# Products of the unit matrix on TensorE between the routing and the first expert

## The reference

```python
h = _layernorm(x) * (1 + ca) + sa
x = x + ga * attention(h)                       # 8 heads, softmax over 1024 positions
h = _layernorm(x) * (1 + cb) + sb
logits = h_flat @ router_w.T                    # 4096 tokens, 8 experts
chosen_e = argmax(softmax(logits)); chosen_p = max(softmax(logits))
pos = cumsum(onehot)[chosen_e] - 1              # place of the token in its expert's rows
kept = pos < 768
buf[chosen_e, pos] = h_flat * kept
hh = gelu(buf @ w1[e] + b1[e])                  # 768x256 by 256x1024
eo = hh @ w2[e] + b2[e]                         # 768x1024 by 1024x256
x = x + gb * eo[chosen_e, pos] * chosen_p * kept
```

## Time and profile before

| | |
|---|---|
| time, median of 3 runs | 975.81 us (975.32 to 976.56) |
| the profiled execution's own time | 975.42 us |
| its span, first to last instruction | 973.7 us |
| PE busy | 865.9 us, 89% of the span |
| DVE, ACT, POOL busy | 670.3, 563.6, 607.0 us |
| mean granted clock of TensorE | 0.943 |
| TensorE idle in one piece at the border of blocks three and four | 25.9 us, to 685.34 us |

### The profile page before, as it was taken

One profiled execution on the slowest core, in us unless ns is written; L12 is line 12 of the kernel. 1 busy time (PEld: TensorE's weight loads), 2 busy tenths in 40 slices (PEclk: granted clock), 3 DMA queues, 4 the chain that ended last, 5 costly groups with the idle time before them and its releaser, 6 DMA issues. The chain is left out here.

```text
span 973.7 us, 20139 instructions
## 1 busy us (share of the span) xinstructions
PE 865.9 (89%) x7974; PEld 605.8 (62%) x7974; DVE 670.3 (69%) x1266; ACT 563.6 (58%) x968; POOL 607.0 (62%) x438
## 2 busy tenths in 40 slices
PE   4895899999999999999999979860799999999995
PEld 1351366666666666666666758760476777677764
DVE  4767887878887878887888609843276567565743
ACT  3641476767676767676767745653447545644650
POOL 5200388888888888888888974786324533452342
PEclk9995699999999999999999989965799999999998
DMA  9911000000000000000000014378434534353110
GB/s 276 335 68 33 1 1 2 3 2 2 2 1 2 2 2 3 2 2 2 2 2 3 2 51 162 120 260 277 145 107 135 183 101 162 129 172 103 43 52 20
DMA packets 52368, 72.32 MB, mean 74 GB/s; under 512 B 11618, under 2 KB 44583, under 8 KB 52048
## 3 DMA queue, kind: packets, MB, share of 16 engines
q1 hardware_dynamic: 42322, 53.93, 16.8%
q0 software_dynamic: 7680, 16.87, 5.3%
q10 hardware_dynamic: 2272, 0.24, 0.2%
HBM read 46.76 MB, written 29.67 MB: 78 GB/s over the span
## 5 line engine op out<-in xcount | busy, mean ns | idle before, releaser
L809 POOL TENSOR_TENSOR prob_lo<-prob 128x1024 f16<-128x1024 f32 x208 | 390.4, 1896 | 120.4 <-ACT prob L781 119.9
L833 DVE TENSOR_REDUCE part_max<-x_ps 128x1 f32<-128x512 f32 x512 | 325.2, 681 | 79.0 <-PE x_ps L730 75.7
L781 ACT ACTIVATE prob<-st_ps 128x512 f32<-128x512 f32 x512 | 281.6, 595 | 114.4 <-PE st_ps L718 108.6
L730 PE MATMUL x_ps<-KX,CQ 98*128 98x512 f16 x512 | 205.0, 405 | 4.0 <-DVE KX L845 1.4
L718 PE MATMUL st_ps<-CQ,KX 99*128 99x512 f16 x512 | 197.2, 386 | 2.8 <-ACT prob L781 1.5
L1304 POOL DMA_INDIRECT out<-yo,xb x48 | 47.7, 994 | 153.4 <-DVE yo L1411 148.5
L756 PE MATMUL acc_ps<-VV,prob 128*128 128x65 f16 x1664 | 128.5, 193 | 2.9 <-POOL prob_lo L809 2.9
L756 PE MATMUL acc_ps<-VV,prob_lo 128*128 128x65 f16 x1664 | 128.1, 193 | 0.0
L756 PEld LDWEIGHTS acc_ps<-VV,prob 128*128 128x128 bf16 x1664 | 116.2, 98 | 18.0 <-DVE both L852 5.0
L756 PEld LDWEIGHTS acc_ps<-VV,prob_lo 128*128 128x128 f16 x1664 | 108.6, 97 | 21.5
L1334 ACT ACTIVATE act_f<-g_ps,cols 128x768 f32<-128x768 f32 x64 | 57.7, 901 | 104.4 <-PE g_ps L1457 103.0
(11 more groups left out here) (172 smaller groups left out, 1256.7 us busy)
## 6 DMA issues: line engine op xcount, KB each, us to landing
w1f<-in_L_ffn_w SPq DMA_DIRECT2D x8, 1024.0 KB, 5.0
w2f<-in_L_ffn_w SPq DMA_DIRECT2D x8, 1024.0 KB
xbuf<-zeros SPq DMA_DIRECT2D x7, 910.0 KB, 17.2
xb<-xbuf SPq DMA_DIRECT2D x8, 780.0 KB
x<-in_L_attn_h_t SPq DMA_DIRECT2D x8, 512.0 KB, 9.0
out<-x SPq DMA_DIRECT2D x4, 1024.0 KB
tbuf<-x SPq DMA_DIRECT2D x4, 1024.0 KB
tbuf<-gb_row SPq DMA_DIRECT2D x4, 1024.0 KB
```

The costliest lines, as they stand in the source:

```text
L730: mm(x_ps[i % 3][:], queries_of[:, n % 2, b * P:(b + 1) * P, j], KX[0:QROWS, n % KRING, f * HALF:(f + 1) * HALF], start=True, stop=True).t ...
L781: nc.scalar.activation(prob[:, k, f * HALF:(f + 1) * HALF], st_ps[i % 2][:], ACT.Exp).then_inc(exp_done, 1)
L809: nc.gpsimd.tensor_tensor(prob_lo[:, k, :], prob[:, k, :], prob_top[:, k, :], ALU.subtract).then_inc(sub_pool, 1)
L833: nc.vector.tensor_reduce(part_max[:, n % 2, j, f:f + 1], x_ps[((n * ST + j) * 2 + f) % 3][:], AX.X, ALU.max).then_inc(smax_done, 1)
```

## The change

Two loops of products are added on TensorE; nothing else differs. The first stands at the end of TensorE's list of the third block, behind the last `positions`: 144 products of `ident16` by `ident16`, read twice side by side (256 columns), written by turns to the two buffers of `oT_ps`. The second stands at the head of TensorE's list of the fourth block, before `turn(0, 0)`: 30 products of `ident16` by `ident16`, read four times (512 columns), all into `y_ps[0]`. Neither waits on a semaphore and neither signals one. What they write is never read: `oT_ps` has been read to the end by then, and `down(0, 0)` starts `y_ps[0]` anew.

```diff
@@ -1216,6 +1216,11 @@
                         turn(n - TURN_LAG)
                     if j == 2 and routed_at(g) is not None:
                         positions(routed_at(g))
+                for _ in range(72):
+                    mm(oT_ps[0][:].rearrange("p k n -> p (k n)"), ident16[:], ident16[:, 0:P].unsqueeze(1).broadcast_to([P, KD, P]),
+                       start=True, stop=True)
+                    mm(oT_ps[1][:].rearrange("p k n -> p (k n)"), ident16[:], ident16[:, 0:P].unsqueeze(1).broadcast_to([P, KD, P]),
+                       start=True, stop=True)
         three.close()
         latents.close()
 
@@ -1473,6 +1478,8 @@
                                       start=c == 0 and f == 0, stop=c == 2 and f == FT - 1)
                     last.then_inc(y_ready, 1)
 
+                for _ in range(30):
+                    mm(y_ps[0][:], ident16[:], ident16[:, 0:P].unsqueeze(1).broadcast_to([P, HALF // P, P]), start=True, stop=True)
                 for r in range(TURNS):
                     turn(0, r)
                 for e in range(E):
```

## The result

The changed kernel takes 978.29 us in the median (977.63 to 979.48, 8 runs) beside 975.95 us of the kernel before on the same chip: ratio 1.0028, interval 1.0018 to 1.0037, or 2.3 us slower. The profiled execution took 979.39 us, its span is 977.7 us.

A forecast was written before the change was run, and what follows sets the result against it. The first expert's start was taken to bound the kernel, any shift passing to the end; second loop 2.1 us late plus 1.8 us slow clock, less 3.2 us gain, gives +0.7 us, 976.5 us; range 974.7 to 978.8 us.

The forecast's parts named there:

- the likeliest case: Whole kernel: first loop free, second loop late and partly slow, clock gain kept; +0.7 us, 976.5 us, 44%.
- This loop costs nothing: First loop, end of block three: drained at 678 us, 2.6 us before GpSimd, so no cost.
- the cover: End of block three: GpSimd's drain ends 2.6 us after the first loop's; without it the loop would cost 18 us.
- My first sign of being wrong: Border to block four: the release moves from 680.8 us, meaning the first loop is too long.
- The pause: Between the loops: TensorE stands still 3.4 to 4.1 us; clock falls before or soon after the second loop starts.
- The second loop: Head of block four: 6.5 us at full clock, ending 2.1 us behind the rows; a slow spell adds 1.8 us.
- The gain: Turning and first 24 g_ps products at full clock: 0.95 and 2.29 us less, sum 3.2 us, passed on undiminished.
- the first rival: Turning's rests for xl: clock falls again, costing 1.6 to 2.3 us in g_ps; 978.1 to 978.8 us, 32%.
- The third sign: First expert: wrong if the shift at its end differs from the shift at g_ps by more than 0.3 us.

The follow-up runs named there:

- the 128-column version: Against the changed kernel: first loop is 288 products of 128 columns, the same columns in twice the instructions; 977.67 us, one run.
- the shorter loop: Against the changed kernel: 112 products in the first loop instead of 144; 976.54 us, ratio 1.0008.
- the half-instruction loop: Against the changed kernel: first loop is 72 products of 512 columns into a_ps, the same columns in half the instructions; 977.40 us, ratio 1.0018.
- the filled: Against the changed kernel: first loop waits for w2l, 64 products; second loop 20; 8 and 10 filler products in the waits for xl; 973.98 us, ratio 0.9980.
- early wide version: Against the changed kernel: first loop 84 products of 512 columns, no wait for w2l; second loop 20; waits for xl filled; 973.50 us, ratio 0.9981.
- late loop: Against the changed kernel: first loop waits until VectorE has made w2l and has 64 products instead of 144; 974.71 us, ratio 0.9989.
- second loop alone: Against the changed kernel: first loop left out, only the 30 products of 512 columns ahead of the first turn; 977.05 us, ratio 1.0013.
- first loop only: Against the changed kernel: second loop left out, only the 144 products of 256 columns ending block three; 977.71 us, ratio 1.0021.
- splits behind: Against the changed kernel: ScalarE's and VectorE's splits of the first expert's weights wait for the first loop's end; 992.82 us, one run.
- other tiles: Against the changed kernel: the first loop's 144 products of 256 columns go to a_ps instead of oT_ps; 978.70 us, one run.

## Why the prediction was right or wrong

The range held the time, and the sign of the likeliest case was right (+0.7 worked out, +2.3 measured), but I had put 68% on a change below 0.2%, it was 0.24 to 0.28%, and the way there was another one. That the time lies in the range is in part luck, as the point on the errors that met shows.

- **"This loop costs nothing": the step that failed.** By its columns the loop is 17 to 18 us long, as the 128-column version shows (17.8 us). In the shape of the change it loses 3.8 us to holes, drops to half clock for 3.4 us more (1.7 us lost), and ends at 684.1 us, after GpSimd. I had named the cover, 2.6 us, and what it costs if it is gone, but took a loop of plain products to run as its columns do. Shown by the shorter loop: 1.7 us for 32 products less. I also took GpSimd's drain as fixed; beside the early first loops it was 0.3 to 1.3 us longer. My first sign of being wrong, a release that moves, came true: 684.35 instead of 680.8 us, 2.0 us of it left when the 1.6 are off.
- **The pause.** I expected 3.4 to 4.1 us and a fall of the clock in it. Because the first loop was late, the pause was 0.3 us and the clock stood. Where the pause did exist (3.06 and 4.51 us, the short and the half-instruction loop), the clock fell as forecast, and the second loop took 8.3 and 9.3 us, of which 8.3 was my value. After pauses of 2.03 and 2.25 us (the filled and the early wide version) it did not fall.
- **The second loop** cost 6.5 us at full clock and began the turn 2.0 us late, by the term of the sum. The page "TensorE: Matmul & The Clock Gate" of the Trainium skill, section "Back-to-back issue gap", with its 131 ns for 512 columns would have made it 3.9 us, an estimate. The trace has 6.63 us for 30 such products, so the measurement decides against it here.
- **The gain** of 3.2 us was right in size wherever the clock stood (late loop, second loop alone) and 1.6 us where it fell.
- **A second fall while the rows are turned,** the first rival, took place, at 695.2 us, and the first 24 products of `g_ps` took 5.6 us, as I had said for that case. Filling the rests is worth 1.7 us, as priced. The time I gave it, 978.1 to 978.8 us, also holds the measured 978.29, but by luck: it had a slow second loop in it, which was not there, and no loss at the border, which was.
- **Which errors met:** +1.4 and +0.6 at the border that I had not, +1.7 from the rival, -1.8 from a second loop that was not slow. From +0.7 this gives +2.6, beside the 2.4 of the profiles.
- **The third sign** was badly put: by the forecast itself the shift shrinks by 2.3 us between the start of `g_ps` and the end of the first expert, so it could not stay within 0.3. Behind the 24th product the shift is 3.95 us (1.6 of them the late clock's) and at the end of the expert's `g_ps` 3.96, so that part of the argument, that all of it passes on, held.

What stays open is the holes' cause. Five kernels have them (changed, first loop only, short, splits behind, other tiles). They begin at times from 664.6 to 667.2 us, but always after the 37th product, some of them with a first rest of only 0.1 us. They are absent with 128 columns, with 512, and with 64 late products of the same shape. The splits, the number of instructions alone and the output buffers are excluded. Full DMA engines are no sufficient cause either, and no necessary one: the late loop ran without holes at a DMA share of 1.02 (670.7 to 676.2 us), and the version with the splits behind had them at 0.49 (666.6 to 678.6 us). Nor does a 16 KB read of TensorE's instructions lie beside them: in the changed kernel these begin at 645.5 and 674.8 us. What it is was not found.

## What to carry to other kernels

Filler on an idle engine is not free up to the barrier merely because its columns fit: leave it a margin, look for its own pauses in the trace, and ask what sets the release: another engine's drain is not a constant. A clock is only worth what runs behind it, so fill every rest between the filler and the dense work, not just the first, and make the last filler end when the data lands and not later. Here the same idea lost 2.3 us as proposed and won 2.9 us once the first loop had slack, the second was as long as the wait, and the rests in the turning were filled.

## What the runs showed of the hardware

- A stream of equal fp16 products stopped "for issue" with 256 columns and ran through with 128 (288 in 17.77 us) and 512, at the same place in the program.
- The 16 KB read of TensorE's instructions in the middle of a load went with a longer load: 5.4 and 5.7 us in the two versions where it lay inside and the turn waited for the rows, 4.5 to 4.6 us where it did not. SyncE's second instruction of that load took 1.6 to 1.9 instead of 0.43 us. Instructions added in one place move that read in another.
- GpSimd's drain over the same scatters took 19.65 to 19.73 us in the six kernels in which TensorE was idle or started late (before, second loop only, the late ones), and 20.0 to 21.0 us in seven with an early first loop, by one trace each. In the eighth, in which the load of the next weights started only at 694.1 us, it took 16.2 us.
- At the start of block three the clock became full at 582 to 586 us in the 14 traces, though TensorE's list up to there is the same in all; between the kernel before and the changed one this alone was worth 1.6 us, about the scatter of the times.
